# State steps in other banks, a rearranged last step and a reordered first step in a chunked linear-attention layer

## The reference

```
xn = layernorm(x)
q, k, v = silu(xn Wq), silu(xn Wk), silu(xn Wv)
per chunk: o = (q k^T * D) v + (q S) * q_decay ;  S = chunk_decay * S + (k * k_decay)^T v
gate = (xn Wg1) Wg2 ;  s = groupnorm_rms(o * sigmoid(gate)) * norm_w @ Wo
f = silu( fp8(xn * scale) fp8(W2 * scale1) / (scale * scale1) )
out = x + s * f
```

## Time and profile before

| | |
|---|---|
| median of 3 runs | 165.73 us (164.69 to 166.13) |
| profiled execution | 165.27 us |
| its span in the trace | 163.5 us |
| busy: TensorE, VectorE, ScalarE, GpSimd | 80%, 67%, 45%, 45% |
| mean granted TensorE clock | 0.922 |

### The profile page before, as it was taken

How to read it: one execution, slowest core, us unless ns; L and a number is a source line. 1 busy time by engine, 2 the same in 40 slices (tenths; PEclk the granted TensorE clock), 3 DMA queues, 4 the chain that set the end, 5 groups by cost and what they waited for, 6 DMA issues and landing times.

```text
span 163.5 us, 7165 instructions
## 1 busy us (share of the span) xinstructions
PE 130.1 (80%) x3114; PEld 110.6 (68%) x3114; DVE 110.1 (67%) x300; ACT 73.1 (45%) x135; POOL 72.8 (45%) x112
## 2 busy tenths in 40 slices
PE   4689793096499997999799979997998996089482
PEld 4579682084399777978787977697677974078460
DVE  1499898234589579948985896589279816833832
ACT  3584961724917566453648344744446440001000
POOL 5707488378145446526652656265246403000300
PEclk9999999569969999999999999999999999858955
DMA  4797000000000000100020010001000100000101
GB/s 138 205 285 227 6 0 6 0 0 0 6 6 4 4 4 0 68 4 4 2 72 0 4 64 8 4 0 66 8 6 4 64 8 32 32 4 4 64 0 64
DMA packets 6846, 6.04 MB, mean 37 GB/s; under 512 B 1376, under 2 KB 6816, under 8 KB 6816
## 3 DMA queue, kind: packets, MB, share of 16 engines
q1 hardware_dynamic: 6816, 5.60, 10.8%
HBM read 3.50 MB, written 2.10 MB: 34 GB/s over the span
## 4 chain that ended last, share of the span: by engine, by line
PE 56%; DVE 24%; issue 9%; ACT 4%; DMA 3%; POOL 2%; SPq 1%; DVEq 0%; ACTq 0%
PE b_q L1031 10%; PE b_o L996 9%; PE b_o L981 5%; DVE probs L626 5%; PE b_x L845 3%; DVE b_x L671 3%; DVE b_x L669 3%; DMA w_f<-in_L_attn_Wv_dram 3%; PE b_k L923 3%; PE b_s L915 3%; PE b_x L1020 3%; DVE sg L711 3%; PE b_o L957 3%; PE b_v L869 2%; PE b_q L856 2%
## 5 line engine op out<-in xcount | busy, mean ns | idle before, releaser
L326 POOL TENSOR_TENSOR e_sum<-e_y,e_magic 128x512 f32<-128x512 f32 x8 | 10.6, 1326 | 26.9 <-DVE e_magic L611 26.9
L1031 PE MATMUL b_q<-wo_scaled,on 128*128 128x256 f32 x60 | 16.0, 411 | 0.8 <-DVE on L690 0.8
L996 PE MATMUL b_o<-probs,v_par 64*32 64x64 f32 x1024 | 16.0, 233 | 0.7 <-issue 0.6
L362 POOL TENSOR_TENSOR y<-sg,x_sb 128x512 f32<-128x512 f32 x7 | 8.9, 1273 | 16.8 <-DVE sg L711 16.8
L334 POOL TENSOR_TENSOR qd<-q_silu,q_decay 128x512 f32<-128x512 f32 x8 | 10.4, 1296 | 12.1 <-ACT q_silu L456 12.1
L658 DVE SCALAR_TENSOR_TENSOR og<-gate_tanh,b_o 128x512 f32<-128x512 f32 x8 | 5.5, 688 | 14.5 <-PE b_o L996 14.5
L996 PEld LDWEIGHTS b_o<-probs,v_par 64*32 64x32 f32 x1024 | 10.8, 111 | 5.9 <-issue 5.2
L869 PE MATMUL b_v<-w_hi,xT_hi 128*128 128x256 f32 x32 | 9.1, 303 | 6.3 <-DVE g1T L621 6.3
L456 ACT ACTIVATE q_silu<-b_q 128x512 f32<-128x512 f32 x8 | 4.8, 601 | 19.0 <-PE b_q L861 19.0
L1031 PEld LDWEIGHTS b_q<-wo_scaled,on 128*128 128x128 f32 x60 | 11.2, 198 | 3.0 <-DVE on L690 1.1
L508 ACT ACTIVATE og_sq<-og 128x512 f32<-128x512 f32 x8 | 5.0, 631 | 16.2 <-DVE og L658 16.2
(11 more groups left out here) (146 smaller groups left out, 388.0 us busy)
## 6 DMA issues: line engine op xcount, KB each, us to landing
out_dram<-y SPq DMA_DIRECT2D x7, 256.0 KB, 2.2
x_sb<-in_L_attn_x_dram SPq DMA_DIRECT2D x4, 384.0 KB, 5.7
x_sb<-in_L_attn_x_dram SPq DMA_DIRECT2D x2, 256.0 KB, 3.7
w_f<-in_L_attn_Wq_dram SPq DMA_DIRECT2D x1, 256.0 KB, 3.0
w_f<-in_L_attn_Wk_dram SPq DMA_DIRECT2D x1, 256.0 KB, 4.7
w_f<-in_L_attn_Wv_dram SPq DMA_DIRECT2D x1, 256.0 KB, 4.9
w_f<-in_L_ffn_input_dram SPq DMA_DIRECT2D x1, 256.0 KB, 2.8
wo_f<-in_L_attn_Wo_dram SPq DMA_DIRECT2D x1, 256.0 KB, 5.4
```

Of the source, the lines that this page charges most:

```text
L326: g.tensor_tensor(e4_sum[:], e4_y[:, n % 2], e4_magic[:], ALU.add).then_inc(s_e4sum, 1)
L362: g.tensor_tensor(y[:, n % 2], sg[:].rearrange("p (s d) -> p s d", s=S), x_sb[:, x_tiles(n), :], ALU.add).then_inc(s_y, 1)
L996: mm = t.matmul(ps_o[32 * r:32 * r + 32, c, z:z + C], v_par[rows, u, blk:blk + 2 * E], probs[rows, r, s, i:i + C], start=(c == 0 and pos(n ...
L1031: mm = t.matmul(dst, on[:, kk, s * P:s * P + P], wo_scaled[:, kk], start=(kk == 0 and (s == 0 or n == STEPS - 1)), stop=(kk == KH - 1), sk ...
```

## The change

1. **Banks.** ps_u moves from b_o into the first quarter of b_q (c = 0) and b_k (c = 1). state_steps(n) moves behind project_v(n + 1); it no longer waits for masks, but for k_nat and both q_par of n + 1. from_state moves behind three of the four from_chunk, which now open the accumulation. transpose_k and project_o wait for the state updates. VectorE does head_norm(n - 1) ahead of the state updates. ffn of step 0 goes into b_q.
2. **Last steps.** Step 7 is written out. It uses banks of its own: sums in b_k, the spread of step 6 in b_v, the last output in b_s. The second half of project_o(5) and head_sums(6) come behind scores(7). The roots of step 6 stand behind the masks of step 7 and are split: a seed and two iterations before gate_o(7), the rest behind it. project_o(6) and product(6) follow. There are 25 keep_warm calls in four places where there were eight in one.
3. **First step.** log_decay is loaded second and x of step 1 ahead of Wv; POOL makes own_head first; ScalarE makes q_decay and k_decay ahead of normalise(0); VectorE makes w_hi(2) and copies kT of step 0; transpose_k(0) and scores(0) come ahead of transpose_x(1), and v of step 1 no longer waits for low_g1(1) (but for low_g1(0)). The gate's weights (wg2) come behind the masks on VectorE. Ten keep_warm become fourteen.
4. og and e4_magic have two buffers each.

```diff
-ps_u = b_o[:].rearrange("p (c z) -> p c z", c=2)[:, :, 256:384].rearrange("p c (k s e) -> p c k s e", k=KH, s=S)
...
-ps_last = [b_q[:, 0:D], b_k[:, 0:D]]
+ps_ffn0 = b_q[:].rearrange("p (s n) -> p s n", s=S)
+ps_u = [b[:, 0:W // 4].rearrange("p (k s e) -> p k s e", k=KH, s=S) for b in (b_q, b_k)]
...
+ps_u_last = [ps_u[1]]
+ps_sum_last = b_k[:, W // 2:W // 2 + C]
+ps_rs_last2 = b_v[:].rearrange("p (k t) -> p k t", k=KH)
+ps_last = [b_s[:, 0:D], b_s[:, 512:512 + D]]
...
 sp.dma_start(x_sb[:, x_tiles(0), :], x_v[:, x_tiles(0), :]).then_inc(s_x[0], 16)
+sp.dma_start(ld_row[:], log_decay.unsqueeze(0).broadcast_to([P, H])).then_inc(s_ld, 16)
 load_w(0, Wq)
 load_w(1, Wk)
+sp.dma_start(x_sb[:, x_tiles(1), :], x_v[:, x_tiles(1), :]).then_inc(s_x[1], 16)
 load_w(2, Wv)
-sp.dma_start(ld_row[:], log_decay.unsqueeze(0).broadcast_to([P, H])).then_inc(s_ld, 16)
-sp.dma_start(x_sb[:, x_tiles(1), :], x_v[:, x_tiles(1), :]).then_inc(s_x[1], 16)
...
+    need(pool, s_e4q, n)
+    g.tensor_tensor(e4_sum[:], e4_y[:, n % 2], e4_magic[:, n % 2], ALU.add).then_inc(s_e4sum, 1)
...
 g.tensor_tensor(w2_m[:], w2_y[:], w2_f32[:], ALU.add).then_inc(s_w2sum, 1)
+decay_q(0)
+norm_factors(2)
 round_y(0)
...
 a.activation(table_load[:, 0:1], eps_col[:, 0:1], ACT.Exp)
 high_w(0)
-high_w(1)
...
 a.activation(k_decay[:], k_logdecay[:], ACT.Exp).then_inc(s_actc, 1)
...
+high_g1(0)
+silu_q(1)
+silu_q_parity(1)
+silu_k(1)
+gate(0)
+act.wait_ge(s_pool, 17)
+silu_v(1)
+normalise(2)
+high_g1(1)
+find_over(0)
+act.wait_ge(s_w2q, 4)
+a.activation(w2_over[:], w2_q[:], ACT.Copy, scale=E4_OVER).then_inc(s_w2q, 1)
+gate(1)
+high_xT(2)
+scale_y(2)
+copy_kT(1)
+find_over(1)
+act.wait_ge(s_dvec, 7)
+silu_ffn(0)
+silu_ffn(1)
+act.wait_ge(s_wo, 48)
+for kk in range(KH):
+    a.activation(wo_scaled[:, kk], wo_f32[:, kk], ACT.Copy, scale=nw_col[:, kk:kk + 1]).then_inc(s_woready, 1)
+square_o(0)
+for n in range(1, STEPS):
+    nxt = known(n + 1)
+    if known(n + 2):
         normalise(n + 2)
     if nxt:
         silu_q(n + 1)
+        high_g1(n + 1)
         silu_q_parity(n + 1)
...
     dve.wait_ge(s_exp, n + 1)
-    need(dve, s_e4q, n)
...
+    need(dve, s_on, n - 1)
+    v.scalar_tensor_tensor(out=og[:, n % 2], in0=gate_tanh[:, n % 2], scalar=1.0, in1=ps_o,
                            op0=ALU.add, op1=ALU.mult).then_inc(s_og, 1)
+def root_seed(n):
...
+def root_step(n, m):
+    dve.wait_ge(s_rs, RS_STEPS * n + 3 * m + 2)
+    v.scalar_tensor_tensor(out=rs_half, in0=og_rs[:], scalar=-0.5, in1=rs_var, op0=ALU.mult, op1=ALU.mult).then_inc(s_rs, 1)
+    dve.wait_ge(s_rs, RS_STEPS * n + 3 * m + 3)
+    v.tensor_tensor(rs_err, rs_half, og_rs[:], ALU.mult).then_inc(s_rs, 1)
+    dve.wait_ge(s_rs, RS_STEPS * n + 3 * m + 4)
+    v.scalar_tensor_tensor(out=og_rs[:] if m < 2 else rs_full, in0=rs_err, scalar=1.5, in1=og_rs[:],
+                           op0=ALU.add, op1=ALU.mult).then_inc(s_rs, 1)
+def root_pair(n):
     dve.wait_ge(s_rs, RS_STEPS * n + 11)
...
     v.tensor_tensor(rs_spread[:], rs_pair.unsqueeze(1).broadcast_to([P, 4, C]),
                     own_block[:].unsqueeze(2).broadcast_to([P, 4, C]), ALU.mult).then_inc(s_spread, 1)
+def rsqrt(n):
+    root_seed(n)
+    for m in range(3):
+        root_step(n, m)
+    root_pair(n)
 def head_norm(n):
     dve.wait_ge(s_rsps, n + 1)
     dve.wait_ge(s_og, n + 1)
     need(dve, s_outps, S * n)
+    v.tensor_tensor(on[:].rearrange("p k (s c t) -> p (k s) c t", s=S, c=2), og[:, n % 2].rearrange("p c (z t) -> p z c t", z=KH * S),
...
+low_w(0)
...
+low_xT(0)
...
+stats(1)
+dve.wait_ge(s_w[2], 16)
+v.tensor_copy(w_hi[:, 2], w_f32[:, 2]).then_inc(s_whi, 1)
+low_w(2)
...
+dve.wait_ge(s_kTps, 1)
+v.tensor_copy(kT[:, 0], ps_kT).then_inc(s_kT, 1)
...
+dve.wait_ge(s_pool, 19)
+dve.wait_ge(s_actc, 5)
+mask(0, 2)
+mask(0, 3)
+low_xT(1)
+mask(0, 0)
+mask(0, 1)
+low_g1(0)
+stats(2)
+exponent(0)
+magic(0)
...
+exponent(1)
+magic(1)
+add_state_mid(0)
+add_state_end(0)
+dve.wait_ge(s_w2sum, 1)
+v.scalar_tensor_tensor(out=w2_q[:], in0=w2_f32[:], scalar=-1.0, in1=w2_m[:], op0=ALU.mult, op1=ALU.add).then_inc(s_w2q, 1)
+low_g1(1)
+put_nan(0)
+dve.wait_ge(s_w2q, 5)
+v.scalar_tensor_tensor(out=w2_fp8[:], in0=w2_over[:], scalar=0.0, in1=w2_q[:], op0=ALU.mult, op1=ALU.add).then_inc(s_w2q, 1)
+stats(3)
+low_xT(2)
...
+for n in range(1, STEPS - 1):
+    rsqrt(n - 1)
+    mask(n, 2)
+    mask(n, 3)
+    low_g1(n + 1)
+    mask(n, 0)
+    mask(n, 1)
+    head_norm(n - 1)
+    add_state_mid(n)
+    add_state_end(n)
+    put_nan(n + 1)
     if known(n + 3):
         stats(n + 3)
     if known(n + 2):
         low_xT(n + 2)
+    gate_o(n)
     if known(n + 2):
         exponent(n + 2)
         magic(n + 2)
         product(n - 1)
...
+n = STEPS - 1
+for r in (2, 3, 0, 1):
+    mask(n, r)
+add_state_mid(n)
+product(n - 2)
+root_seed(n - 1)
+root_step(n - 1, 0)
+root_step(n - 1, 1)
+gate_o(n)
+root_step(n - 1, 2)
+root_pair(n - 1)
+head_norm(n - 1)
+rsqrt(n)
+product(n - 1)
+head_norm(n)
...
+    pe.wait_ge(s_kT, n + 1)
+    if known(n + 1):
+        pe.wait_ge(s_k, n + 2)
+        pe.wait_ge(s_qpar, 2 * (n + 2))
+    u_ps = ps_u if known(n + 1) else ps_u_last
...
     if c == 0 and pos(n) == 0:
         return
+    pe.wait_ge(s_qd, n + 1)
     if c == 0:
...
 pe.wait_ge(s_pool, 6)
+keep_warm(14, ps_score[1])
 transpose_x(0)
...
+transpose_k(0)
+scores(0)
 transpose_x(1)
...
+pe.wait_ge(s_g1w, 3)
+project_g1(0)
+project_q(1)
+project_k(1, 0)
+project_k(1, 1)
+project_v(1, 0)
+project_v(1, 1)
+state_steps(0)
+pe.wait_ge(s_g2w, 5)
+gate(0)
+project_g1(1)
+from_chunk(0, 0, 0)
+transpose_x(2)
+from_chunk(0, 0, 1)
+gate(1)
+transpose_k(1)
+from_chunk(0, 1, 0)
+from_state(0, 1)
+pe.wait_ge(s_hsum, 1)
+for half in range(KH):
+    mm = t.transpose(ps_spread[:, half], head_sum[:, half], ident[:])
+mm.then_inc(s_pec, 1)
+pe.wait_ge(s_w2q, 6)
+ffn(0)
+ffn(1)
+from_chunk(0, 1, 1)
+head_sums(0)
+for n in range(1, STEPS - 1):
+    scores(n)
+    project_q(n + 1)
+    project_g1(n + 1)
+    project_k(n + 1, 0)
+    project_k(n + 1, 1)
+    spread_rs(n - 1)
+    project_v(n + 1, 0)
+    project_v(n + 1, 1)
+    state_steps(n)
+    gate(n + 1)
+    from_chunk(n, 0, 0)
...
     if known(n + 2):
         transpose_x(n + 2)
...
+    from_chunk(n, 0, 1)
+    transpose_k(n + 1)
+    from_chunk(n, 1, 0)
+    from_state(n, 0)
+    from_state(n, 1)
+    ffn(n + 1)
+    from_chunk(n, 1, 1)
+    if n == 1:
+        pe.wait_ge(s_woready, 2)
+    project_o(n - 1, 0)
+    if known(n + 2):
+        project_o(n - 1, 1)
         head_sums(n)
+n = STEPS - 1
+scores(n)
+project_o(n - 2, 1)
+head_sums(n - 1)
+state_steps(n)
+keep_warm(4, b_v)
+from_chunk(n, 0, 0)
+from_chunk(n, 0, 1)
+from_chunk(n, 1, 0)
+from_state(n, 0)
+from_state(n, 1)
+from_chunk(n, 1, 1)
+keep_warm(5, b_v)
+head_sums(n)
+keep_warm(4, b_v)
+spread_rs(n - 1)
+project_o(n - 1, 0)
+project_o(n - 1, 1)
+keep_warm(12, b_v)
+spread_rs(n)
+for s in range(S):
+    project_o(n, s)
```

More of the change, by code:

```diff
@@ L529, in _ @@
             a.activation(table_load[:, 1:2], eps_col[:, 0:1], ACT.Silu)
-            act.wait_ge(s_small, 32)
-            scale_y(0)
             silu_k(0)
-            normalise(1)
             act.wait_ge(s_qps, 1)
@@ L536, in _ @@
             silu_q_parity(0)
-            copy_kT(0)
-            high_xT(1)
+            normalise(1)
+            act.wait_ge(s_small, 32)
+            scale_y(0)
             act.wait_ge(s_pool, 16)
             silu_v(0)
+            high_xT(1)
             silu_q(0)
             scale_y(1)
-            for n in range(STEPS):
-                nxt, cur = known(n + 1), known(n)
-                if known(n + 2) and n > 0:
+            high_g1(0)
[25 more added lines that the diff above has]
+                if known(n + 2):
                     normalise(n + 2)
@@ L773, in _ @@
             v.tensor_tensor(wg2_stack[low_rows], wg2_f32[low_rows], wg2_hi[low_rows].bitcast(F32), ALU.subtract).then_inc(s_g2w, 1)
-            low_xT(1)
-            dve.wait_ge(s_pool, 18)
-            dve.wait_ge(s_actc, 5)
-            for n in range(0, STEPS + 1):
-                nxt, cur, back = known(n + 1), known(n), known(n - 1)
-                if back and nxt:
-                    rsqrt(n - 1)
-                if cur:
-                    mask(n, 2)
-                    mask(n, 3)
-                if nxt and n > 0:
-                    low_g1(n + 1)
-                if cur:
-                    mask(n, 0)
-                    mask(n, 1)
-                if n == 0:
-                    exponent(0)
-                    magic(0)
-                    low_g1(0)
-                    stats(2)
-                if cur:
-                    add_state_mid(n)
-                    add_state_end(n)
-                if back and not nxt:
-                    rsqrt(n - 1)
-                if n == 0:
-                    dve.wait_ge(s_w2sum, 1)
-                    v.scalar_tensor_tensor(out=w2_q[:], in0=w2_f32[:], scalar=-1.0, in1=w2_m[:], op0=ALU.mult, op1=ALU.add).then_inc(s_w2q, 1)
-                    put_nan(0)
```

(24 more changed lines are left out.)

270 lines of the change are left out of this document (91 added, 179 removed).

## The result

The changed kernel takes 158.03 us (median of four, 157.42 to 159.34) against 165.55: a ratio of 0.956, 95% interval 0.949 to 0.964. It is faster, but by half of what was forecast (150.0), and 3 us above the upper end of the range. The profiled execution spans 156.1 us. Some executions of one kernel take 1.5% or more longer than its fastest: ratios and intervals leave them out, medians hold them, and the profiled executions of experiments 1, 3 and 4 are among them, so that their lines are read for waits and positions and not for total times.

A forecast was written before the change was run, and what follows sets the result against it. TensorE, busy 80%, was taken to bound the kernel, with waits for masks, start and tail: 40.3 + 14.6 + 58.0 + 11.8 + 23.2 = 147.9 us of span, forecast as 150.0, range 146.5 to 155.0.

The forecast's parts named there:

- (a): Steady steps: state_steps, moved to b_q and b_k behind project_v, starts near 96.5 with k_nat ready at 95.38, without a wait.
- (b): Steady steps: VectorE's masks (7.46 us) and TensorE's way to the gate (7.5) meet; the 0.86 us wait goes, nothing replaces it.
- (c): Steady steps: head_norm ahead of state updates; transpose_k's new wait hidden by 0.4 us, own_mid and own_end ready before from_state.
- (d): Steady steps: two og and two magic buffers remove waits that nobody stands in.
- the check of the sum: A steady step rebuilt from its parts: 14.1 us plus some 0.4 of issue gaps as before, against the forecast 14.5.
- Step 1: Head sums of step 0 to step 1's product: 13.9 us with full clock, 15.2 without; 14.6 taken.
- Start: Up to step 0's head sums: scores at 16.5, gate idle 3.5 us for its weights, head sums at 40.3 instead of 44.32.
- the 2.7 that the sum put on the casts: Start: POOL's operations slow the gate-weight casts, so they end at 28.0 us rather than 25.3.
- Tail: Last chunk of step 6 to the end: 23.2 us instead of 29.8, roots holding gate_o(7) by 0.3, last stage at full clock.
- Rivals: 1: start gains nothing, 154 us, 0.15; 2: tail clock falls, 155, 0.10; 3: start at upper clock, casts slip through, 147, 0.13.
- Rival 4: Steady steps: state hand-over to VectorE, POOL and from_state becomes the bound; slower than before, 168 us, chance 0.02.
- Its partial form: Steady steps: the state hand-over costs 1 us a step, 156 us in all; chance 0.03.

The follow-up runs named there:

- experiment 1: The changed kernel run again without any edit, as the measure for others: 158.39 us, ratio 0.951 to the kernel before.
- experiment 3: Changed kernel with state_steps back ahead of spread and v, in its new banks: 156.05 us, ratio 0.940 to the kernel before.
- experiment 4: Kernel before the change, with low_g1(n + 1) ahead of masks 2 and 3: 169.72 us, ratio 1.016 to the kernel before.
- experiment 2: Changed kernel with low_g1(n + 1) ahead of masks 2 and 3 on VectorE: 152.88 us, ratio 0.921 to the kernel before.
- experiment 5: Changed kernel with the gate's four casts and subtraction moved right behind low_g1(0) on VectorE: 156.38 us, ratio 0.949 to the kernel before.
- experiment 6: Changed kernel without the 25 warm-up calls of the last step: 157.88 us, ratio 0.958 to the kernel before.
- gap filled: Changed kernel with six warm-up calls ahead of ffn(1) and six ahead of head_sums(0): 156.74 us, ratio 0.955 to the kernel before.
- all together: Changed kernel with low_g1 ahead of masks 2 and 3, earlier gate casts, twelve calls around ffn(1) and head_sums(0), last-step roots' twelve calls cut to eight: 149.82 us, 0.905.
- the same, gap not filled: Changed kernel with low_g1 first, earlier gate casts and eight calls for twelve in the last roots, without calls ahead of ffn(1) and head_sums(0): 151.49 us, 0.916.
- experiment 7: Changed kernel with ten warm-up calls at the start in place of fourteen: 157.77 us, ratio 0.956 to the kernel before.

## Why the prediction was wrong, point by point

- **Steady steps, (a)**: right. state_steps has no wait in its new place (its 0.7 in the last step is a stop at issue).
- **Steady steps, (b)**: the step that failed. "They meet, so the 0.86 goes and nothing takes its place" counted TensorE's way to the gate with v right behind spread, and VectorE's to the last mask, but not the operation between the masks: v waits for low_g1, which VectorE gives at product + 6.15, where spread is done at product + 5.2. In the kernel before, state_steps and its wait lay on top of this one, low_g1 done at 95.9 and v starting at 96.6:

```profile
95.48 0.42 DVE L621 TENSOR_TENSOR g1T<-b_v,g1T 32x256 fp32r<-32x256 f32 x1
```
```profile
96.62 0.28 PE L869 MATMUL b_v<-w_hi,xT_hi 128*128 128x256 f32 x1
```

  The change takes that cover away. It costs 4.9 us in five waits, 0.97 each where 0.86 had gone; experiment 2 takes them away and gets 5.1. The upper bound of the sum, 61.5 for "the wait comes back elsewhere", allowed for such a wait, but at 0.86 and without the stops: measured 63.2.
- **(c), (d)**: right: neither transpose_k nor from_state waits for VectorE or POOL.
- **Issue gaps**: the check of the sum had "some 0.4" a step "as before", but TensorE's trace before has 0.37 us of them in the four steps together (one, at 103.24), 0.23 in step 6 (at 133.37) and none in the tail. By taking 15.38 and 12.6 over, the sum held these and no more. Measured: 1.1, 0.4 and 1.9 us. With the excess the stretches come out nearly: 58.0 + 3.9 + 0.7 = 62.6 for 63.2; 11.8 + 1.0 + 0.2 = 13.0 for 13.1; 23.2 + 1.9 = 25.1 for 24.8. The 0.6 that is left in the four steps is not accounted for.
- **Step 1**: 15.2 at half clock in part, the upper of the two values given (17.1 in the execution of experiment 1); with the full clock 14.7, and 14.0 with low_g1 first too, where I had 13.9.
- **Start**: scores at 15.9 (16.5), gate waiting for wg_stack, head sums at 39.7 (40.3): right. The wait for wg_stack is 2.52, not 3.5. The subtraction waited beside POOL too (1.44 against 0.42). By that the rule of the Trainium skill, "GPSIMD Engine Reference", Specifications, on two SBUF inputs agrees with the trace here, where I had called it mixed. The head sums came 2.2 to 2.7 earlier in experiment 5, near the 2.7 that the sum put on the casts; but that edit made casts and subtraction 2.1 us shorter and put them 2 us earlier in the queue at once, so it does not measure the casts alone.
- **Tail**: mechanism right (spread(6) without a wait, project_o(7) at 1.00, the warm-ups ending 0.9 after rs_spread). gate_o(7) ended 10.8 behind the last chunk and not 8.6: it waited for TensorE, with 1.9 us of stops at issue ahead of it, and not for the roots. The sum charged the twelve calls 1.2 us and let them hold the clock; experiment 6 shows neither.
- **Rivals**: none had this mechanism. Rival 4 looked at the right edge, the new place of state_steps, but downstream of it, at the hand-over. Its partial form came nearest in time (156, with 0.03), by a size of 1 us a step that fits and a cause that does not.

## What to carry to other kernels

When a wait is taken away, list every semaphore that the work behind it waits for, and when each comes; a wait that never shows in the table may be covered by the one that goes. Ask this of the instruction that moves up, not only of the one that moves. The order of two producers on one engine is right only for one order of their consumers: change one, and try the other.

## What the runs showed of the hardware

**TensorE's stops at issue lie on a grid.** Matmuls started before each stop that is not at the start, in the order of time:

```
before                    1985  2743
changed, first            1854  1980  2357  2734  2859  2986
changed, again             722  1098  1477  1979  2357  2735  2859  2986
ten calls at the start    1099  1476  1979  2357  2734  2859  2986
gap filled                1100  1476  1603  1981  2357  2735  2987  3113
all together              1099  1602  1981  2358  2734  2988  3114
the same, gap not filled   722  1476  1979  2357  2734  2859  2986
```

(Left out are idle times that the profile calls issue but that follow the end of another engine's work by 0.10 us each: in "all together" four of 0.17 and one of 0.48 ahead of the gate, behind the last mask, and three such in the kernel without the filling; in the kernel before, 0.45, 1.65 and 2.05 us at 25.5, 38.2 and 44.3, the last one in the earlier trace rows, behind low_g1, put_nan's result and ScalarE's square. They are waits: each stands at the first matmul of a group, where the program waits for a semaphore, while every stop listed here falls inside a group; and all but one of them, 228, lie 19 or more matmuls off the grid that follows.) From 722 to 2986 are 2264 matmuls, 18 times 125.8, and every other number stands on that grid to within nine, most to within two, in kernels whose instructions differ by 8 and 24 matmuls ahead of it. The page of the profile has 25 transfers of 0.41 MB on an instruction queue, 16.4 KB each; 0.46 MB over 7273 instructions are 63 bytes for one, so by this estimate some 260 in a transfer: 126 matmuls, as many weight loads, and waits. That the stop is the wait for the next transfer is worked out from this, not shown by itself. The Trainium skill, "Runtime: NRT & Kernel Launch", Instruction fetch mechanics, has such blocks of 16 KiB or 256 instructions, and calls the cost of crossing one mostly hidden. The length agrees; the cost does not: 0.15 to 1.4 us at a crossing, 3 to 5 us in an execution of the changed kernels and 0.6 us in the kernel before. So some 3 us of stops came with the change, against its gain; that more closely packed matmuls bring them is not shown. The stops are seen where the 126 matmuls ahead went by in 2.5 to 4.3 us with the stop, most of them 32 and 64 wide, and not where they took 4.5 or more, but for 2859 (4.7 to 5.0) and for 1098 in experiment 3 (5.2). Not every short block has one: the kernel before took 3.3 to 3.8 us for four without, the changed kernel's first execution 2.9 to 3.4 us for four, the one up to 722 among them. Why a crossing costs 0.6 us in one execution and 1.2 in another of the same kernel (2986) stays open, and so does why a short block has none.

**The clock at the start.** The page of the profile gives 1.00 for the first slices of every run, and that is not the rate there: in the kernel before, the windows 2 to 7 and 8 to 12 us say 1.00 while the warm-ups come 0.21 us apart and four transposes take 1.11 us, against 0.11 and 0.66 at the upper rate. So the start is read from durations. By these the rate rose between 5.0 and 8.0 us in eleven of the twelve profiled executions, TensorE having worked from 2.1 us on without a pause. In the kernel before the ten calls ended at 6.8 us without a rise; then came the pause of 2.11 us, and the lower rate stayed until 15.2. In experiment 4 the rise came at 5.0, but the pause of 3.16 us that followed ended at the lower rate. In experiment 7 it came at 5.3, and the pause of 1.63 us kept the upper rate.

**The clock at the end.** In experiment 6, 3.77 us of matmuls at the lower level ended with the upper one granted for the next stage.
